# Distance keys made as a guest of the first stage, and the last state space weighed by GpSimd and summed by TensorE

## The reference, cut to what matters

```
x = x + 0.5 * local_ffn(norm(x))      # 2 layers: window attention, then a gated feed-forward
x = x + attention(norm(x))            # 8 heads with relative positions
x = x + 0.5 * local_ffn(norm(x))      # the same weights again
x = x + 0.5 * experts(norm(x))        # 64 experts, the best 8 per token, and a shared one
x = x + state_space(norm(x))          # 256 channels, 16 states
```

## Time and profile before

| | us |
|---|---|
| median of 3 runs | 4794.54 (4786.48 to 4795.5) |
| profiled execution, its own time | 4797.14 |
| its span, first to last instruction | 4795.1 |
| PE busy | 3971.9 (83%) |
| DVE busy | 3014.1 (63%) |
| ACT busy | 2772.1 (58%) |
| POOL busy | 2071.1 (43%) |
| mean granted TensorE clock | 0.933 of 2.4 GHz |

### The profile page before, as it was taken

How to read it: one execution, slowest core, us unless ns; L and a number is a source line. 1 busy time by engine, 2 the same in 40 slices (tenths; PEclk the granted TensorE clock), 3 DMA queues, 4 the chain that set the end, 5 groups by cost and what they waited for, 6 DMA issues and landing times. The chain is left out here.

```text
span 4795.1 us, 54417 instructions
## 1 busy us (share of the span) xinstructions
PE 3971.9 (83%) x17076; PEld 2403.6 (50%) x17076; DVE 3014.1 (63%) x5743; ACT 2772.1 (58%) x6174; POOL 2071.1 (43%) x1350
## 2 busy tenths in 40 slices
PE   6787898888888888888987989878888888888846
PEld 3445554555545554455544555445554555445412
DVE  4326666667576674766657666666757667477464
ACT  4466557565576565665566655756557556565332
POOL 2104254544364441744436434454436444175334
PEclk9799999999999999999999999999999999999867
DMA  3020013111131111210121101311113111121212
GB/s 104 1 90 1 17 56 115 36 48 37 38 123 39 38 46 60 93 49 25 59 87 61 55 29 54 112 38 49 34 42 123 39 38 46 60 90 52 78 49 76
DMA packets 188824, 274.01 MB, mean 57 GB/s; under 512 B 23448, under 2 KB 102900, under 8 KB 188532
## 3 DMA queue, kind: packets, MB, share of 16 engines
q1 hardware_dynamic: 186340, 268.72, 17.6%
q10 hardware_dynamic: 2192, 1.70, 0.1%
HBM read 215.54 MB, written 54.79 MB: 56 GB/s over the span
## 5 line engine op out<-in xcount | busy, mean ns | idle before, releaser
L604 POOL TENSOR_TENSOR work<-work 128x512 f32<-128x512 f32 x512 | 667.9, 1305 | 1211.9 <-DVE work L664 1124.3
L1515 POOL TENSOR_TENSOR work<-work,minus_half 128x8 f32<-128x8 f32 x256 | 473.9, 1865 | 537.2 <-DVE work L1498 534.2
L664 DVE SCALAR_TENSOR_TENSOR work<-work,psum 128x512 f32<-128x512 f32 x528 | 362.3, 687 | 419.6 <-ACT work L596 418.6
L1618 ACT ACTIVATE work<-psum,work 128x128 f32<-128x128 f32 (+1 forms) x1024 | 392.6, 397 | 387.8 <-DVE work L1640 387.4
L572 PE MATMUL psum<-work,w_up 128*128 128x512 f32 x1024 | 545.6, 616 | 64.2 <-DVE work L664 60.4
L596 ACT ACTIVATE work<-psum 128x512 f32<-128x512 f32 x528 | 315.9, 599 | 434.1 <-PE psum L572 427.0
L578 PE MATMUL psum<-work,w_down 128*128 128x512 f32 x1024 | 542.3, 612 | 3.4 <-POOL work L604 3.4
L1443 PE MATMUL psum<-wqkv,xn 128*128 128x512 f32 x768 | 389.4, 634 | 56.0 <-PEq L387 39.4
L1583 PEld LDWEIGHTS psum<-work 128*128 128x128 f32 x3072 | 388.9, 197 | 61.3 <-issue 47.9
L1583 PE MATMUL psum<-work 128*128 128x64 f32 x3072 | 412.0, 279 | 9.2 <-ACT work L1605 8.6
L1572 PE MATMUL psum<-ident,work 128*128 128x128 f32 x1536 | 250.3, 288 | 151.9 <-ACT work L1618 116.4
(11 more groups left out here) (238 smaller groups left out, 8476.5 us busy)
## 6 DMA issues: line engine op xcount, KB each, us to landing
work<-expert_weight_rows SPq DMA_DIRECT2D x1024, 128.0 KB, 2.9
position_scores<-work SPq DMA_DIRECT2D x64, 768.0 KB, 3.5
work<-position_scores SPq DMA_DIRECT2D x64, 512.0 KB, 3.8
work<-state_readout_rows SPq DMA_DIRECT2D x72, 256.0 KB, 4.4
rows<-state_readout_rows SPq DMA_DIRECT2D x32, 256.0 KB, 4.0
sq<-state_readout_rows SPq DMA_DIRECT2D x24, 256.0 KB, 4.2
rows<-in_L_attn_q SPq DMA_DIRECT2D x8, 256.0 KB, 3.6
expert_weight_rows<-work SPq DMA_DIRECT2D x16, 128.0 KB, 2.3
```

The lines of the kernel that those rows point to most:

```text
L604: pool.tensor_tensor(h, h, self.weights[p % self.SLOTS], ALU.mult).then_inc(self.gated, 1)
L664: v.scalar_tensor_tensor(out=self.gate_h[p % 3][0:rows], in0=self.tanh_h[p % self.turns][0:rows], scalar=1.0, in1=bank(b, self.ups[p % sel ...
L1515: pool.tensor_tensor(half, half, b.minus_half[:].broadcast_to([128, LH]), ALU.pow).then_inc(self.inv_norm, 1)
L1618: ins = self.nc.scalar.activation(out[:, x, -n:] if t else out[:, x], self.scores(m)[:, x], ACT.Exp, bias=self.neg_max[i % 2][:, slot:slot ...
```

## The change

`rest_of_weights` becomes a guest class with nine steps: step 0 transposes the centroids, steps 1 to 8 make one head's keys each, in banks 6 and 7 by turns. The first stage of group 0 calls them by the new shares `FIRST`: none in slots 0 and 1, three in slot 2 (rounds 2, 5, 7), two in each of slots 3, 4 and 5 (rounds 3 and 7). A head's ScalarE copy is written at the same place of ScalarE's queue. The token load and the entry norm get an empty guest. Because the stage now has a guest, its `beside.rest` makes a block, empty here.

In the state space alone, GpSimd makes the product with C as it does beside a host; TensorE adds the states of all 16 in banks 6 and 7 by a product with the identity (`sum_states`), placed in its queue two scans after the pair was scanned; there are four pairs of state buffers (`turns`) in place of two. `sums` is not zeroed there, and L965 reads the two banks.

```diff
+class RestOfWeights:
+    STEPS = 1 + AH
+    BANKS = (6, 7)
+    def tensor(self, pe, k):
+        nc, b, h = self.nc, self.b, k - 1
+        if k == 0:
+            pe.wait_ge(self.later_loaded, 16 * self.transfers)
+            nc.tensor.transpose(bank(b, self.BANKS[1])[:, 0:EXPERTS], self.centroids, b.ident[0:EXPERTS, 0:EXPERTS]).then_inc(self.turned, 1)
+        else:
+            if h == 1:
+                pe.wait_ge(self.copied, 1)
+            if h >= 2:
+                pe.wait_ge(self.keys_copied, h - 1)
+            out = bank(b, self.BANKS[h % 2])
+            nc.tensor.matmul(out, self.w_rel[:, 0, h * AD:(h + 1) * AD], self.pos[:, 0, :], start=True, stop=False)
+            nc.tensor.matmul(out, self.w_rel[0:64, 1, h * AD:(h + 1) * AD], self.pos[0:64, 1, :], start=False, stop=True).then_inc(self.products, 1)
+    def scalar(self, act, k):
+        h = k - 1
+        if k >= 1:
+            act.wait_ge(self.products, h + 1)
+            self.nc.scalar.copy(self.b.rel_k[:, h, :], bank(self.b, self.BANKS[h % 2])).then_inc(self.keys_copied, 1)
+    def vector(self, dve, k):
+        if k == 0:
+            dve.wait_ge(self.turned, 1)
+            self.nc.vector.tensor_copy(self.b.centroids_t[:], bank(self.b, self.BANKS[1])[:, 0:EXPERTS]).then_inc(self.copied, 1)
...
@@ first_and_third
-    beside = Beside(Experts(nc, b, sems.stage(f"{name}_experts"), carve, weight_rows, alone=not early) if late else None)
+    beside = Beside(Experts(nc, b, sems.stage(f"{name}_experts"), carve, weight_rows, alone=not early) if late else guest and guest(sems.stage("rest")))
     if load:
-        load(beside)
+        load(Beside(None))
...
@@ StateSpace
+        if alone:
+            self.state_pairs += [chunked(), chunked()]
+        self.turns = len(self.state_pairs)
...
             spread(bank(b, self.BANKS[j % 2]), j // 2).then_inc(self.spread_b, 1)
+            if self.alone and j >= 5 and j % 2 == 1:
+                self.sum_states(pe, (j - 5) // 2)
+        elif self.alone and k == self.STEPS - 3:
+            self.sum_states(pe, STATES - 2)
         elif k == self.STEPS - 2 and self.alone:
+            self.sum_states(pe, STATES - 1)
...
+    def sum_states(self, pe, n):
+        pe.wait_ge(self.weighted, n + 1)
+        for c in range(2):
+            ins = self.nc.tensor.matmul(bank(self.b, self.BANKS[2 + c]), self.b.ident[:], self.state_pairs[n % self.turns][:, c], start=n == 0, stop=n == STATES - 1)
+        ins.then_inc(self.added, 1)
...
-        elif k == 5:
+        elif k == 5 and not self.alone:
             pool.memset(self.sums, 0.0).then_inc(self.added, 1)
         elif 3 <= j <= self.SCANS + 1 and j % 2 == 1:
             n = (j - 3) // 2
-            if not self.alone:
-                self.weight(pool, pool, n)
+            self.weight(pool, pool, n)
+            if self.alone:
+                return
...
-                if i >= 4 and i % 2 == 0:
-                    dve.wait_ge(self.added, i // 2)
+                if i >= 2 * self.turns and i % 2 == 0:
+                    dve.wait_ge(self.added, i // 2 - self.turns + (1 if self.alone else 2))
...
-            if self.alone and j >= 3 and j % 2 == 1:
-                self.weight(dve, v, (j - 3) // 2)
         elif k == self.STEPS - 2 and self.alone:
-            dve.wait_ge(self.added, 1 + STATES)
+            dve.wait_ge(self.added, STATES)
...
-                gated.link(v.scalar_tensor_tensor(out=self.conv[:, c], in0=self.x_c[:, c], scalar=vec(b, ("Dp", c)), in1=self.sums[:, c],
+                gated.link(v.scalar_tensor_tensor(out=self.conv[:, c], in0=self.x_c[:, c], scalar=vec(b, ("Dp", c)), in1=bank(b, self.BANKS[2 + c]),
...
@@ LocalFfn
+    FIRST = ({}, 0, 3, 2, 2, 2)
...
-        shares = self.CARRIED if self.carry else self.AHEAD
+        shares = self.CARRIED if self.carry else self.AHEAD if self.entered else self.FIRST
...
-                        if k in self.Q0_AT:
+                        if self.entered and k in self.Q0_AT:
...
@@ build_program
-                        transfers=(later, later_loaded))
-        rest_of_weights(nc, b, sems.stage("rest"), later_loaded, len(later))
+                        transfers=(later, later_loaded), guest=lambda sem: RestOfWeights(nc, b, sem, later_loaded, len(later)))
```

More of the change, by code:

```diff
@@ L303, in weights @@
         return later
[L306 to L330, removed]
@@ new lines, with __init__, gpsimd, sync @@
+class RestOfWeights:
+    STEPS = 1 + AH
+    BANKS = (6, 7)
+    def __init__(self, nc, b, sem, later_loaded, transfers):
+        self.nc, self.b, self.later_loaded, self.transfers = nc, b, later_loaded, transfers
+        self.turned, self.copied, self.products, self.keys_copied = sem("centroids_turned"), sem("centroids_copied"), sem("products"), sem("keys_copied")
+        self.pos, self.w_rel, self.centroids = staged(b)
+    def tensor(self, pe, k):
[20 more added lines that the diff above has]
+            self.nc.vector.tensor_copy(self.b.centroids_t[:], bank(self.b, self.BANKS[1])[:, 0:EXPERTS]).then_inc(self.copied, 1)
+    def gpsimd(self, pool, k):
+        pass
+    def sync(self, sp, k):
+        pass
@@ L885, in gpsimd @@
             n = (j - 3) // 2
-            if not self.alone:
-                self.weight(pool, pool, n)
+            self.weight(pool, pool, n)
+            if self.alone:
+                return
             pool.wait_ge(self.weighted, n + 1)
             pool.wait_ge(self.added, n + 1)
-            pool.tensor_tensor(self.sums, self.sums, self.state_pairs[n % 2], ALU.add).then_inc(self.added, 1)
+            pool.tensor_tensor(self.sums, self.sums, self.state_pairs[n % self.turns], ALU.add).then_inc(self.added, 1)
     def vector(self, dve, k):
@@ L951, in vector @@
                     at = slice(q * SEQ, (q + 1) * SEQ)
-                    ins = v.tensor_tensor_scan(self.states[i % 4][:, at], self.decays[i % 2][:, at], drive[:, at], 0.0, ALU.mult, ALU.add)
+                    ins = v.tensor_tensor_scan(self.state_pairs[i // 2 % self.turns][:, i % 2, at], self.decays[i % 2][:, at], drive[:, at], 0.0, ALU.mult, ALU.add)
                 ins.then_inc(self.scanned, 1)
@@ L1273, in ffn_stage @@
     if not carry and not entered:
-        norm_block(nc, b, prefixed("entry"), b.x[:], b.y[:], beside)
+        norm_block(nc, b, prefixed("entry"), b.x[:], b.y[:], Beside(None))
     LocalFfn(nc, b, prefixed("passes"), space, carry, ahead, entered, tail).run(beside, transfers)
@@ L1903, in _ @@
                         self.project_gpsimd(pool, 0, t)
-                    beside.gpsimd(pool, upto=2)
+                    if self.entered:
+                        beside.gpsimd(pool, upto=2)
                 for r in R:
@@ L1937, in _ @@
                             self.tail.vector_done(dve)
-                        if step in self.Q0_VECTOR:
+                        if self.entered and step in self.Q0_VECTOR:
                             beside.vector(dve, upto=self.Q0_VECTOR[step])
```

5 lines of the change are left out of this document (2 added, 3 removed).

## The result

The changed kernel takes 4749.33 us (median of 4 runs, 4746.45 to 4761.93), the kernel before beside it 4792.85 (4786.48 to 4795.5): ratio 0.9901, 95% interval 0.988 to 0.9923. The forecast was 4748 us with a range of 4738 to 4763. The profiled execution took 4749.3 us with a span of 4747.2; the forecast for it was 4750.1.

A forecast was written before the change was run, and what follows sets the result against it. No single engine bounds the whole: TensorE alone at the low clock bounds the keys' block, VectorE the last state space. Gains of 22.4 and 24.6 us, 47.0, take 4797.14 to 4750.1 profiled; predicted 4748 us, range 4738 to 4763.

The forecast's parts named there:

- The keys' block leaves 32.2 us: First stage's end: the 32.5 us block of the keys goes, less 0.27 us for the new empty block.
- A head takes 1.95 us inside: First stage, TensorE: a head's two products take 1.95 us at 2.4 GHz, against 3.9 us at the low clock.
- rival B: First stage: the keys stay at the low clock inside it, 15.6 us more, total 4763 us; chance 0.07.
- The guest adds 9.8 us: First stage: the eight heads' delays of TensorE, each less the idle time there, sum to 9.8 us; bounds 1.6 and 20.3.
- Copies at nothing: First stage, ScalarE: seven of eight key copies priced at nothing; uncovered they would cost 4.1 us.
- rival C: First stage: nothing is hidden, every head and copy adds, 20.3 us, total 4758 us; chance 0.15.
- Rival D: First stage, slots 2 to 5: low-clock heads make the host miss rounds, 71.5 us, total 4809 us, slower; chance 0.02.
- 25.6 us by the scans' pitch: Last state space, VectorE: scans follow every 1.89 us, so the last ends at 4673.3 instead of 4698.9, 25.6 us gained.
- Rival A: Last state space: TensorE's sums stay at the low clock, 4.9 us a pair for 3.78, total 4764 us; chance 0.10.
- The end 0.5 gained: Last state space, last scan to L965: 4.7 us becomes 4.4 or 6.3; 0.5 gained, bounds 1.5 gained, 1.6 lost.
- First scan to gating 66 instead of 90: Last state space: the stretch from the first scan to L965 should last 66 us instead of 90.
- Part two, 24.6 us: Last state space: 25.6 us from the scans, less 1.5 for low-clock sums, plus 0.5 at the end, gives 24.6 us.

The follow-up runs named there:

- rest_keys: The changed kernel with all guest shares at zero, so the stage's closing block makes all nine steps: 4766.29 us, ratio 0.9915 to the kernel before.
- two_pairs: The changed kernel with two buffer pairs instead of four in the last state space: 4788.4 us, ratio 0.9972 to the kernel before.
- best: The changed kernel plus fillers in the last state space's prelude, VectorE weighing its last pair, and guest shares 3, 3, 3, 0: 4749.33 us, ratio 0.9887.

## Why the prediction was right

- *The keys' block leaves 32.2 us:* right. The stage without keys, 87.3, and 32.5 of block less 0.3 of empty block make 119.5; with the block it took 119.6 (`rest_keys`), 120.2 and 120.6.
- *A head takes 1.95 us inside:* 2.0, and rival B is out (1.02 and 1.12 a product, clock 0.96).
- *The guest adds 9.8 us:* 5.5 in the changed kernel's profile, 9.3 in its second, 7.9 on average over the eight profiles with these shares. By single heads (starts of the row behind each, less before's): head 0 adds 134.57 - 129.26 = 5.31 to 3.3 that was there already, so 2.0 (forecast 1.95); heads 1 and 2 bring it to 154.66 - 148.21 = 6.45, 1.1 (forecast 1.7); head 3 to 166.71 - 161.05 = 5.66, a gain of 0.8 (forecast a loss of 1.2), since before had a low stretch ahead of it (around 155 us) that this execution has not; heads 4 and 5 to 196.05 - 188.06 = 7.99, 2.3 (forecast 3.35); head 6 leaves it at 203.56 - 195.58 = 7.98, 0 (forecast 0); then the twelve products of the last mix run at the high level, 3.37 us where before they took 4.75, and it falls to 208.71 - 202.10 = 6.6; head 7 and what follows add 1.6 (forecast 1.6). Head 0, where nothing of the host's hid it, and head 7 were right. The sum held the clock of the host's own products fixed, and that step was mis-sized: 4.3 us too dear here, 0.5 in the other execution. The guest keeps the last mix at the high level in every profile, and a low stretch behind head 2 takes more than that away again in five of nine. The 3.4 us by which this execution reached the stage late cancelled most of the miss, by luck.
- *Copies at nothing:* not tested alone; rival C (20.3 us for the guest) is out with 5.5 to 9.3 for products and copies together. Rival D is out; its eight heads of 8.9 us come to 71.2, not 71.5, which changes nothing.
- *25.6 us by the scans' pitch:* right, first scan to last 58.96 us where 31 x 1.89 = 58.6; the low-clock loss was 0.4, not 1.5, as only the first pair's sums ran slow (3.35 us; the second pair's took 1.88). Rival A is out with four buffer pairs; `two_pairs` comes part of the way to its clock (0.73 granted), in a state space that waits.
- *The end 0.5 gained:* from the last scan's end (4650.99 + 1.26) to L995 it is 4.51 us (forecast 4.4, before 4.7), and the two products with `ssm_out_w` run at the high level, so L995 to L1000 takes 4.07 instead of 5.15 us. That makes 1.3 gained, near the upper bound. The old 4.7 was not a clean measure, as it held the 1.1 us by which VectorE's last product was slowed.
- *First scan to gating 66 instead of 90:* 64.7.
- *Part two, 24.6 us:* 23.7, but with a term that the forecast did not have. The scans gave 25.2 and the end 1.3 us, and the prelude, priced at nothing with all that keeps its instructions, took 2.9 back.
- *The middle within 3 us:* 0.3 in this pair of profiles, but over 14 profiles it spreads over 22 us.
- *The range:* its lower gain of 39 us does not follow from the stated bounds, which add up to 12 + 25.6 - 2.4 - 1.6 = 33.6; the measured gain of 43.5 lies inside either.

The mechanisms were the ones predicted: the keys' work at the high level and half hidden, the scans at their own pitch. That the sum came out within 1 us of the profiled time is partly luck. The guest came out 4.3 us cheaper than forecast, the late landmark cost 3.4 and the prelude 2.9, and the middle happened to agree.

## What to carry to other kernels

A block in which one engine works alone is worth moving under a stage that has room, and twice so where the block stands at the low clock and the host does not: here 32.5 us of block became 5.5 to 9.3. The first load into such a host finds idle time (7.0 of 24.6 us here), a second of the same size hardly any (1.7), and costs 12.1 to 15.9 us for 16.5 of products. Where the load stands matters for the host's clock too: one head ahead of the last mix kept it at the high level, and `best`, which moved it away, lost by it. When a sum is handed on to another engine, give the buffers the depth of the hand-over: with two pairs instead of four the same division of work was slower than the old one.

## What the runs showed of the hardware

- The granted clock does not follow TensorE's busy share alone: 32.18 of 33.8 us busy at 0.51 in the closing block of `rest_keys`, 39.78 of 65 us at 0.92 in the last state space. Which property of the block's products (float32, alternating 128 and 64 rows) keeps it low was not tried.
- Two float32 products in a place where TensorE had idled changed the clock of the twelve behind them: the last mix took 3.37 or 3.38 us in the nine profiles with a head ahead of it (idle for at most 0.53 us just before it), and 4.75 to 5.49 in the five without (idle for 2.05 to 2.44 us).
- Two state spaces with the same instructions get different clocks: the median record of the sums is 1057 ns in `two_pairs` and 592 in the kernel after. In both TensorE waits 1.5 us for a scan (once in 3.78 us after, twice in 6.83 in `two_pairs`). That the slow sums keep the clock low by stretching the pair fits this, but no run tests it.
- VectorE's scan, with one input in SBUF and one in PSUM, takes the same 673 to 674 ns with and without GpSimd's product beside it; its product of two SBUF inputs took 2.29 us instead of 1.22 beside GpSimd's addition.
- The same instructions, from the attention's start to the last state space, took 4330.9 to 4353.2 us over 14 profiled executions.
